# Dense mixture of experts: who rounds the gelu outputs and who takes the remainders

## The reference, cut to what matters

```python
x = x + 0.5 * ffn(layernorm(x), ...)          # first half layer
x = x + retention(layernorm(x), ...)
x = x + 0.5 * ffn(layernorm(x), ...)          # second half layer, same weights

def ffn(x, ...):                               # x: (4, 1024, 128)
    x = x + attention(layernorm(x)) @ Wo       # 16 heads of 8
    m = layernorm(x)                           # 4096 tokens of 128
    probs = softmax(m @ Wg)                    # 8 experts
    wts, idx = top_k(probs, 2); wts = wts / sum(wts)
    h1 = gelu(einsum('td,edf->etf', m, W1) + b1)      # 8 experts, 512 hidden units
    ye = einsum('etf,efd->etd', h1, W2) + b2
    return x + sum of wts * ye over the two chosen experts
```

## Time and profile before

| | us |
|---|---|
| Median of three runs (lowest, highest) | 2535.62 (2533.4, 2536.08) |
| The profiled execution: time | 2533.75 |
| The profiled execution: span, first to last instruction | 2532.0 |

### The profile page before, as it was taken

One profiled execution on the slowest core, in us unless ns is written; L12 is line 12 of the kernel. 1 busy time (PEld: TensorE's weight loads), 2 busy tenths in 40 slices (PEclk: granted clock), 3 DMA queues, 4 the chain that ended last, 5 costly groups with the idle time before them and its releaser, 6 DMA issues.

```text
span 2532.0 us, 39142 instructions
## 1 busy us (share of the span) xinstructions
PE 2241.1 (89%) x12680; PEld 1039.6 (41%) x12680; DVE 2155.8 (85%) x2995; ACT 1663.6 (66%) x3025; POOL 825.2 (33%) x877
## 2 busy tenths in 40 slices
PE   2899999999997998899884999999999978999998
PEld 1222222222224776677661222222222226777776
DVE  5889889899964999999657898898899928999999
ACT  1588888788886555555431788788888875555553
POOL 1211221210102666666420201202100005667667
PEclk7799999999998999999895999999999998999999
DMA  2110111101000000010001101100100000111001
GB/s 99 31 48 19 48 31 28 45 25 36 23 2 34 34 34 34 38 63 34 1 9 54 33 22 32 33 27 27 38 17 27 3 2 34 72 39 42 38 38 42
DMA packets 43903, 84.46 MB, mean 33 GB/s; under 512 B 12112, under 2 KB 25680, under 8 KB 41680
## 3 DMA queue, kind: packets, MB, share of 16 engines
q1 hardware_dynamic: 43728, 82.32, 9.8%
HBM read 66.55 MB, written 15.73 MB: 32 GB/s over the span
## 4 chain that ended last, share of the span: by engine, by line
PE 55%; DVE 15%; issue 12%; POOL 11%; ACT 6%; SPq 1%; DMA 1%; POOLq 0%; DVEq 0%; ACTq 0%
PE ps L1189 20%; PE ps L1162 14%; PE ps L1176 7%; POOL hp L528 7%; DVE nmax L832 6%; PE ps L1299 4%; ACT pbuf L657 3%; PE ps L1321 3%; POOL acc L546 3%; DVE hp L998 3%; ACT ct L637 2%; PE ps L1103 2%; PE ps L1132 1%; DVE hp L1002 1%; DVE tmp L968 1%
## 5 line engine op out<-in xcount | busy, mean ns | idle before, releaser
L832 DVE TENSOR_REDUCE nmax<-ps 128x2 f32<-128x1024 f32 x1024 | 1212.4, 1220 | 167.2 <-PE ps L1176 160.2
L657 ACT ACTIVATE pbuf<-ps 128x512 f32<-128x512 f32 x2048 | 1084.0, 601 | 261.9 <-PE ps L1162 255.7
L1162 PE MATMUL ps<-qs,ks 51*128 51x512 bf16 x2048 | 614.9, 386 | 18.2 <-ACT pbuf L657 10.7
L1176 PE MATMUL ps<-ks,qs 48*128 48x512 bf16 x2048 | 523.2, 400 | 83.2 <-DVE nmax L832 48.8
L668 ACT ACTIVATE hr<-ps,small 128x512 f32<-128x512 f32 x512 | 344.1, 688 | 356.9 <-PE ps L1299 167.6
L1189 PE MATMUL ps<-pbuf,vst 128*32 128x512 f32 x4096 | 547.7, 607 | 11.8 <-ACT ct L637 11.8
L528 POOL TENSOR_TENSOR hp<-hr,hp 128x512 fp32r<-128x512 f32 x256 | 429.4, 1678 | 301.1 <-DVE hp L998 301.1
L1321 PE MATMUL ps<-hp,wp 128*128 128x512 f32 x1536 | 448.1, 401 | 24.3 <-DVE tmp L968 17.2
L1299 PE MATMUL ps<-mtp,wp 128*128 128x512 f32 x1536 | 457.5, 407 | 0.0
L998 DVE CAST hp<-hr 128x512 fp32r<-128x512 f32 x512 | 420.6, 843 | 22.3 <-ACT hr L668 15.1
L1162 PEld LDWEIGHTS ps<-qs,ks 51*128 51x128 bf16 x2048 | 154.9, 94 | 663.6 <-ACT pbuf L657 609.3
(11 more groups left out here) (141 smaller groups left out, 1280.4 us busy)
## 6 DMA issues: line engine op xcount, KB each, us to landing
qkv<-w_scratch SPq DMA_DIRECT2D x16, 2048.0 KB, 7.1
part_scratch<-qkv SPq DMA_DIRECT2D x32, 384.0 KB, 2.6
ks<-part_scratch SPq DMA_DIRECT2D x384, 32.0 KB
qs<-part_scratch SPq DMA_DIRECT2D x384, 32.0 KB
w_piece<-in_w SPq DMA_DIRECT2D x16, 256.0 KB, 2.7
x<-in_x SPq DMA_DIRECT2D x4, 512.0 KB, 5.1
qs<-nm_scratch SPq DMA_DIRECT2D x128, 6.0 KB
result<-x SPq DMA_DIRECT2D x8, 256.0 KB, 2.0
```

The lines of the kernel that those rows point to most:

```text
L657: act.activation(pbuf[:, step % 3, u, :], ps[:, s_bank(i), :], ACT.Exp, scale=SCALE).then_inc(s_taken, 1)
L832: dve.tensor_reduce(nmax[:, half, kh, 4 * j + 2 * u:4 * j + 2 * u + 2], ps[:, bank:bank + 2, :], AX.X, ALU.max, negate=True).then_inc(max_ ...
L1162: mm(ps[:, bank, :], ks[G % 3][rows, u // 2, s % 8 * P:(s % 8 + 1) * P], qs[G % 3][rows, u // 2, s // 8 * 512:s // 8 * 512 + 512], start=True,
L1176: last = mm(ps[:, bank + hb, :], qs[G % 3][rows, pair, first:first + P], ks[G % 3][rows, pair, kh * 512:kh * 512 + 512], start=True, stop= ...
```

## The change

The rounded half of a gelu output is no longer cast by DVE. For even blocks ACT casts it (an activation Copy from `hr` to `hp[0]`, issued behind the gelu of the odd block that follows), for odd blocks POOL does. All 32 remainders are made on DVE, one for each block, in order, and counted by one semaphore, `hl_ready`, for which the gelu four blocks later and the down product wait. The rounded halves are counted by `hh_even` and `hh_odd`, for which DVE waits. The waits for a free buffer of `hp` (`down_done`) move with the casts to ACT and POOL.

```diff
@@ sum_experts (POOL)
                 for k in range(1, BLOCKS, 2):
-                    pool.wait_ge(hh_ready, n * 32 + (k + 1))
-                    pool.tensor_tensor(hp[1][k % 8], hr[k % 4], hp[0][k % 8].bitcast(F32),
-                                       ALU.subtract).then_inc(hl_odd, 1)
+                    pool.wait_ge(gelu_done, n * 32 + (k + 1))
+                    if k >= 8 or not first:
+                        pool.wait_ge(down_done, n * 32 + (k - 7))
+                    apart()
+                    pool.tensor_copy(hp[0][k % 8], hr[k % 4]).then_inc(hh_odd, 1)
@@ gelus (ACT)
+                first = isinstance(c, int) and c == 0 and layer == 0
                 for k in range(BLOCKS):
                     act.wait_ge(h_filled, n * 32 + (k + 1))
-                    if k >= 4 or not (isinstance(c, int) and c == 0 and layer == 0):
-                        act.wait_ge(hh_ready, n * 32 + (k - 3))
-                        act.wait_ge(hl_odd if k % 2 else hl_even, n * 16 + (k // 2 - 1))
+                    if k >= 4 or not first:
+                        act.wait_ge(hl_ready, n * 32 + (k - 3))
                     act.activation(hr[k % 4], ps[:, k % 4, :], ACT.Gelu_apprx_tanh,
                                    bias=b1_sb[:, k // 4, k % 4:k % 4 + 1]).then_inc(gelu_done, 1)
+                    if k % 2:
+                        act.wait_ge(gelu_done, n * 32 + k)
+                        if k >= 9 or not first:
+                            act.wait_ge(down_done, n * 32 + (k - 8))
+                        act.activation(hp[0][(k - 1) % 8], hr[(k - 1) % 4], ACT.Copy).then_inc(hh_even, 1)
                     for f in after.get(k, ()):
                         f()
@@ mix, one (DVE)
-                        dve.wait_ge(gelu_done, n * 32 + (k + 1))
-                        if k >= 8 or not first:
-                            dve.wait_ge(down_done, n * 32 + (k - 7))
-                        dve.tensor_copy(hp[0][k % 8], hr[k % 4]).then_inc(hh_ready, 1)
-                        if k % 2:
-
-                            dve.wait_ge(hh_ready, n * 32 + k)
-                            dve.tensor_tensor(hp[1][(k - 1) % 8], hr[(k - 1) % 4],
-                                              hp[0][(k - 1) % 8].bitcast(F32), ALU.subtract).then_inc(hl_even, 1)
+                        dve.wait_ge(hh_odd if k % 2 else hh_even, n * 16 + (k // 2 + 1))
+                        dve.tensor_tensor(hp[1][k % 8], hr[k % 4], hp[0][k % 8].bitcast(F32),
+                                          ALU.subtract).then_inc(hl_ready, 1)
@@ down (PE)
-                pe.wait_ge(hh_ready, n * 32 + (k + 1))
-                pe.wait_ge(hl_odd if k % 2 else hl_even, n * 16 + (k // 2 + 1))
+                pe.wait_ge(hl_ready, n * 32 + (k + 1))
```

More of the change, by code:

```diff
@@ L301, in macaron @@
         w_written, w_spread = sem("w_written"), sem("w_spread")
-        mtf_ready, down_done, hh_ready, hl_even, hl_odd = (sem("mtf_ready"), sem("down_done"), sem("hh_ready"),
-                                                           sem("hl_even"), sem("hl_odd"))
+        mtf_ready, down_done, hh_even, hh_odd, hl_ready = (sem("mtf_ready"), sem("down_done"), sem("hh_even"),
+                                                           sem("hh_odd"), sem("hl_ready"))
         h_filled, gelu_done, tmp_ready, tmp_added, out_turned, x_final = (
```

## The result

| | us |
|---|---|
| Before, median of four runs | 2535.35 |
| After, median of four runs (lowest, highest) | 2509.21 (2506.51, 2513.33) |
| Ratio, with its 95% interval | 0.9899 (0.9882 to 0.9917) |
| The profiled execution after: time, span | 2508.23, 2506.5 |

The change makes the kernel 1.0% faster, some 26 us. The forecast was 2464, a gain of 71. The measured time lies just inside the range (2510), at the place of the rival called lockstep, and the gain is under half of the forecast one: the forecast was wrong in size. That it still falls inside the range is partly luck, as the part on the prediction shows.

What follows compares the result with a forecast made beforehand. DVE was taken as the bound, holding ACT and PE. Savings of 34.8 and 28.2 us in the inner chunks, 5.6 in first chunks and 2.8 at the ends made 71.4 us: 2464, range 2436 to 2510.

Steps and rivals of the forecast that it cites:

- lockstep: Rival, inner chunks: even casts sit behind ACT's table loads and DVE stands for each, 53.2 us a chunk, 2510; chance 0.21.
- DVE's sum: Inner chunk: DVE's own work 37.5 us, 45.6 with port waits, 48.1 with 2.5 of idle time.
- term for port waits: Inner chunk: DVE waits 8.1 us for the port it shares with POOL, 0.42 of POOL's 19.3 us.
- The share of 42%: Waiting of DVE's casts before the change, 12.6 us a chunk, as part of POOL's pure time of 29.8.
- ACT's copy: Sixteen copies a chunk on ACT at 0.63 us each, beside PE as a sum and costed at nothing.
- I allow 1.4 us a chunk: Around block 8 ACT falls some 4 us behind; PE or DVE stands there for 1.4 us a chunk.
- The 49.5 us a chunk: Forecast length of an inner chunk: DVE's 48.1 us with 1.4 of standing.
- Late by 0.7 and caught up again: POOL's cast and addition order takes 3.5 us where an odd block is due after 2.8, within the ring's slack.
- A floor of 47.5: PE's own pace for an inner chunk, 47.5 us; as a rival that PE alone sets, 2436 to 2450, chance 0.20.
- The first chunks at 48.8: First chunk of each mixture falls from 51.25 and 51.91 to 48.8 us, saving 2.5 and 3.1.
- The end of the mixture: After PE's last down products, the end is no longer held by the last remainders: 1.4 us saved, twice.
- The port rival: Rival called slower: all of POOL's 19.3 us lands on DVE, 56.8 us a chunk, 2556; chance 0.09.

Runs made afterwards that it cites:

- even_dve: Changed kernel with the even casts back on DVE, each just before its remainder, and ACT as before the change: 2568.98 us, ratio 1.0143.
- all_pool: Changed kernel with the even casts on POOL as well, so all 32 casts a chunk are there: 2632.83 us, ratio 1.0394.
- fin9: Changed kernel with DVE's finish of the chunk before after block 9 in place of block 11: 2487.48 us, ratio 0.9817.
- best_w24: copy_own_fin9 with the last two routing steps on DVE after blocks 23 and 24 in place of 24 and 25: 2485.77 us, ratio 0.9802.
- gate23: Changed kernel with the last routing steps on DVE after blocks 21, 22 and 23 in place of 22, 24 and 25: 2532.49 us, ratio 0.9988.
- add_later: Changed kernel with POOL's additions, but the last of a chunk, issued behind the cast of the next odd block: 2529.24 us, ratio 0.9983.
- copy_own_fin9: Changed kernel with ACT's even-block copy directly behind its own gelu and DVE's finish after block 9: 2468.54 us, ratio 0.974.
- best_unrolled: copy_own_fin9 with DVE's hardware loop over chunks 1 to 6 written out in both mixtures: 2458.37 us, ratio 0.9704.

## Why the prediction was wrong, point by point

- DVE's sum. The prices held: the removed work, the remainders, the rest. The term for port waits (8.1 us) was too large: DVE's busy time is 40.1 us, 2.6 over the 37.5. In this loop POOL works while DVE stands and waits, so its time does not lie on DVE; it lies in front of it. The share of 42% was read in a loop where DVE was idle for only 2.5 us a chunk.
- ACT's copy: forecast 0.63, measured 0.624 us (line 676). Costing it at nothing was the failed step. As a sum it is hidden (37.3 of 51.9 us), but its place in the queue is not. "I allow 1.4 us a chunk" stood for the whole of ACT's burst; measured, taking the table loads away gives 39 us, 2.9 us for each of twelve inner chunks, and the copy's order alone 30 us. The 49.5 us a chunk were 45.6 of DVE's work and 3.9 of waiting (2.5 and 1.4); measured in the first mixture are 40.1 and 12.5. So the waiting was short by 8.6 us, and the port term, too large by 5.5, hid most of that: luck.
- POOL. "Late by 0.7 and caught up again" was wrong: DVE waits 6.5 us a chunk for POOL's casts, because the addition ahead of them waits for DVE's mixing (108.2 us in six chunks) and the cast behind it is then late for a remainder that DVE must take before anything else.
- PE stands idle for 3.3 to 3.9 us a chunk, where the sum had 2.0 over PE's floor, and the clock was no term at all: 0.5 us a chunk in the first mixture, 1.6 in the second.
- A floor of 47.5 against 48.1 measured. The first chunks at 48.8 against 50.2 and 49.6. The end of the mixture came out as forecast: from the last up product to the turn of the sum 9.35 us before (the earlier trace rows lies in it), 7.96 after, 1.4 less.
- The second mixture's loop turns, some 4 us each on DVE, could not be read from before.
- The lockstep rival named the right mechanism for half of it (even casts behind table loads) and gave 2510. That the number fits is partly luck as well: it was 48.1 us of DVE and 5.1 behind ACT, where 40.1 and 4.9 are measured, and 6.5 behind POOL, which it did not have. I held DVE's own late work for its cover; the two-sided chain between DVE and ACT around block 8 showed the opposite. The port rival did not happen in the changed kernel, but it did in even_dve and all_pool, both slower than before.
- Of the signs: gelu's waits for the remainder fell from 71.0 to 26 us, just above the 25 named; casts and copies had their prices; remainders took 732 ns, just under the 750 named; the chunks of 49 to 50 us did not come. The sign against it was there too: DVE behind ACT's copy by 4.9 us a chunk, near the 5 named for lockstep.

## What to carry to other kernels

When a full engine is relieved, the next bound can be, as here, not the next sum but the distance between fixed places in two in-order queues: write down for each waiting product which step of which queue it needs, and what stands ahead of that step. A short operation that others need belongs directly behind its input, ahead of long work in the same queue; here that order was worth 30 us and the change itself 26. And a step that is moved ahead delays all that it passes: the same kind of move gave 22 us at one place (fin9) and cost 17 at another (best_w24).

## What the runs showed of the hardware

- Behind stalls of PE of 1.1 to 2.2 us the granted clock sometimes went to its lower level, 1.2 GHz, for a few us (0.67 in a stretch of four us), at a cost of about 2 us each (a chunk of 53.94 us beside one of 51.90); behind equal stalls in neighbouring chunks it did not. In gate23 the clock of the six chunks was 0.97 and in the changed kernel 0.99, with the stall at block 15 as long (12.0 and 11.9 us in six chunks).
- An addition on POOL and a remainder on DVE lengthen each other: with the addition moved out of DVE's waiting, the remainder's mean went from 732 to 873 ns (add_later).
- In the changed kernel DVE stood 4.0 to 4.3 us at the jump back to the head of a long loop in the second mixture, and not in the first. Once the loop was written out, the two chunks of 55.0 and 53.9 us (copy_own_fin9) took 49.3 (best_unrolled). The kernel before had the same loop and showed no such stop. A transfer of 0.01 MB on an instruction queue lies in the stop; that it is the cause is not shown.
